# Two decoder layers on one core: more buffers for the split probabilities, and another order of the second phase

## The reference

```
x += tanh(g0) * fp8_product(ln(x), ctx)                      # 128-blocks, quantised and back
x += tanh(f0) * ternary_linear(rms(ln(x)) in 8 bits, W)      # one scale over all rows
x += tanh(g1) * attention(q=ln(x), k=ctx, v=ctx, 8 heads)    # softmax(q^T k / sqrt(d)) over 1024
x += tanh(f1) * sum_e combine[:, e] * (ln(x) @ Wa[e] @ Wb[e])  # top 2 of 8 experts, rank 128
```

## Time and profile before

| | us |
|---|---|
| median of 3 runs | 2032.5 (2029.92 to 2034.0) |
| the profiled execution | 2032.83 |
| its span, first to last instruction | 2031.0 |
| PE busy | 1856.8 |
| DVE busy | 1542.6 |
| ACT busy | 1265.5 |
| POOL busy | 773.8 |

### The profile page before, as it was taken

The page is one execution under the profiler, slowest core; times in us unless marked ns, Lnnn a source line. Parts: engine busy times, 40 slices in busy tenths (PEclk is TensorE's granted clock), DMA queues, the critical chain, the costliest instruction groups (busy, mean ns, idle before and its releaser), DMA issues.

```text
span 2031.0 us, 26460 instructions
## 1 busy us (share of the span) xinstructions
PE 1856.8 (91%) x8968; PEld 838.4 (41%) x8968; DVE 1542.6 (76%) x2386; ACT 1265.5 (62%) x2045; POOL 773.8 (38%) x1100
## 2 busy tenths in 40 slices
PE   1699999894799999999999999999999999999997
PEld 0244444341344444444444444444444444444443
DVE  8899999888777777777777777777777777777662
ACT  4698898666556566656555565656565665555650
POOL 3555565333333333333333333333333333333320
PEclk9999999997999999999999999999999999999999
DMA  9687876796878888887788787888878878888772
GB/s 213 160 208 205 220 204 182 193 228 186 159 150 166 167 164 158 164 168 161 157 165 168 161 159 151 166 167 162 160 156 168 167 152 165 163 171 160 126 145 63
DMA packets 923975, 340.50 MB, mean 168 GB/s; under 512 B 849728, under 2 KB 898880, under 8 KB 923840
## 3 DMA queue, kind: packets, MB, share of 16 engines
q1 hardware_dynamic: 923840, 338.81, 79.6%
HBM read 93.36 MB, written 33.55 MB: 62 GB/s over the span
## 4 chain that ended last, share of the span: by engine, by line
DVE 21%; ACT 20%; issue 20%; POOL 10%; PE 7%; DMA 5%; SPq 0%; ACTq 0%; DVEq 0%; POOLq 0%
ACT slot L885 9%; DVE tiny L1586 7%; ACT arena L872 6%; POOL tiny L710 5%; DVE tiny L1220 4%; POOL tiny L708 4%; DVE slot L1591 3%; DMA probs<-slot 3%; ACT tiny L864 3%; DVE arena L1601 2%; ACT slot L909 2%; DVE slot L1559 2%; DMA slot<-slot 2%; DVE slot L1648 1%; DVE slot L1553 1%
## 5 line engine op out<-in xcount | busy, mean ns | idle before, releaser
L1591 DVE SCALAR_TENSOR_TENSOR slot<-arena,tiny,slot 128x1024 f16<-128x1024 f32 x256 | 328.2, 1282 | 306.0 <-ACT slot L885 305.9
L885 ACT ACTIVATE slot<-arena,tiny 128x1024 f16<-128x1024 f32 x256 | 293.6, 1147 | 174.1 <-POOL tiny L710 155.0
L1083 PE MATMUL sc<-arena,slot 128*128 128x512 f16 x1536 | 371.2, 382 | 19.2 <-ACT arena L872 17.0
L708 POOL TENSOR_SCALAR tiny<-tiny 128x1 f32<-128x1 f32 x256 | 100.1, 391 | 689.8 <-ACT arena L872 689.8
L1586 DVE TENSOR_REDUCE tiny<-sc 128x1 f32<-128x1024 f32 x256 | 306.5, 1207 | 16.5 <-PE sc L1083 15.1
L872 ACT ACTIVATE arena<-sc,tiny,head_tab 128x1024 f32<-128x1024 f32 x256 | 308.1, 1204 | 8.6
L864 ACT ACTIVATE tiny<-tiny,head_tab 128x1 f32<-128x1 f32 x256 | 73.9, 289 | 338.1 <-DVE tiny L1586 338.0
L1083 PEld LDWEIGHTS sc<-arena,slot 128*128 128x128 f16 x1536 | 150.1, 98 | 204.8 <-ACT arena L872 19.5
L1104 PE MATMUL accs<-probs,arena 128*128 128x512 f16 x512 | 196.9, 385 | 23.3 <-issue 21.1
L1106 PE MATMUL accs<-probs,arena 128*128 128x512 f16 x512 | 196.8, 384 | 0.0
L1105 PE MATMUL accs<-probs,arena 128*128 128x512 f16 x512 | 196.6, 384 | 0.0
(11 more groups left out here) (214 smaller groups left out, 2900.9 us busy)
## 6 DMA issues: line engine op xcount, KB each, us to landing
arena<-in_x SPq DMA_DIRECT2D x32, 512.0 KB, 4.2
x_scratch<-arena SPq DMA_DIRECT2D x32, 512.0 KB, 3.7
slot<-x_scratch SPq DMA_DIRECT2D x32, 512.0 KB, 4.1
slot<-in_ctx SPq DMA_DIRECT2D x32, 512.0 KB, 4.5
out<-arena SPq DMA_DIRECT2D x31, 512.0 KB, 3.4
slot<-in_L_ffn_Wa SPq DMA_DIRECT2D x12, 512.0 KB, 5.0
slot<-in_L_ffn_Wb SPq DMA_DIRECT2D x9, 512.0 KB, 4.9
wb_hi<-in_ctx SPq DMA_DIRECT2D x64, 64.0 KB, 2.5
```

What stands on the lines that cost most here:

```text
L885: act.activation(high, full, ACT.Identity, scale=rinv[c % 4][:]).then_inc(s_ph.sem, 1)
L1083: mm = pe.matmul(sc[:, c % 2, h * HALF:(h + 1) * HALF], q[i][:, c * P:(c + 1) * P], k[j][:, h * HALF:(h + 1) * HALF], start=start, stop=stop)
L1591: dve.scalar_tensor_tensor(out=low, in0=full, scalar=rinv[c % 4][:], in1=high, op0=ALU.mult, op1=ALU.subtract).then_inc(s_pl.sem, 1)
```

## The change

Three SBUF tensors of 128 x 1024 f32 are added (`late0` to `late2`). Room for them comes from the argument `dynamic_dma_scratch_size=4096` of the program, which makes the reserved descriptor scratch smaller. `P2` then has four buffers for all tiles and `PF` three; the semaphores of the probability transposes become four, and the waits of `exp` and `prob_high` follow: `exp(n, c)` waits for `prob_low` of the chunk three before, `prob_high(n, c)` for the transpose of the chunk four before. A wait of `finish_x3` in tile 0 goes, since tile 0 no longer borrows x3's buffer for it. The order of all five lists in the loop changes. In the steady rounds the new lists are (the tile is n where none is given):

The diff, with unchanged lines left out and indents shortened:

```diff
...
+late = [sb(f"late{i}", [P, D]) for i in range(3)]
...
-P2, T42 = [slot[i][:].bitcast(F16) for i in (12, 13)], slot[10][:].bitcast(F16)
+P2 = [t[:].bitcast(F16) for t in (slot[12], slot[13], late[0], late[1])]
+T42 = slot[10][:].bitcast(F16)
...
-P2_FIRST = P2 + [slot[i][:].bitcast(F16) for i in (10, 11)]
...
-PF, X3 = (pf[:, 0], pf[:, 1]), (pf[:, 2], pf[:, 3])
-PF_FIRST = PF + X3
+PF, X3 = (pf[:, 0], pf[:, 1], late[2][:]), (pf[:, 2], pf[:, 3])
+PF_FIRST = PF + X3[1:]
...
-        full, both = PF_FIRST[c % 4], P2_FIRST[c % 4]
+        full = PF_FIRST[c % 4]
...
-        full, both = PF[c % 2], P2[c % 2]
+        full = PF[(KB * n + c) % 3]
+    both = P2[c % 4]
...
-s_pt = signal("s_pt0", 16 * KB // 2), signal("s_pt1", 16 * KB // 2)
-s_pt_first = signals("s_pt_first", 4, 32)
+s_pt = signals("s_pt", 4, 32)
...
-        turned = s_pt_first[c % 4] if n == 0 else s_pt[c % 2]
...
-          .then_inc(turned.sem, 16)
+          .then_inc(s_pt[c % 4].sem, 16)
...
+        if quant:
+            load_x1(n + 2)
...
-        if is_x(n + 2) and n >= -1:
-            load_k(n + 2)
-        if cur:
-            turn_probs(n, 1)
-        if is_x(n + 2) and n >= 1:
-            load_x1(n + 2)
...
+            turn_probs(n, 1)
+        if quant:
+            load_k(n + 2)
+        if cur:
...
-            turn_probs(n, 3)
...
+        if cur:
+            turn_probs(n, 3)
...
+            turn_probs(n, 6)
...
-        if cur:
-            turn_probs(n, 6)
...
+        if prev:
+            ln_factors(n - 1, l4_st, l4_p, mv4, a4, rs4, nb4)
+        if cur:
+            row_factor(n, 2)
...
-        if prev:
-            ln_factors(n - 1, l4_st, l4_p, mv4, a4, rs4, nb4)
-        if cur:
-            row_factor(n, 2)
+        if cur:
+            row_factor(n, 3)
+            row_factor(n, 4)
...
-        if cur:
-            row_factor(n, 3)
-            row_factor(n, 4)
-        if prev and cur:
-            hidden_low(n - 1, 0)
...
+            hidden_low(n - 1, 0)
+        if cur:
+            row_factor(n, 7)
+        if prev and cur:
...
-        if cur:
-            row_factor(n, 7)
...
-        elif c >= 2:
-            act.wait_ge(s_pl.sem, s_pl.at(n, c - 1))
+        elif n == 1 and c == 0:
+            act.wait_ge(s_pl.sem, s_pl.at(0, KB - 1))
...
-            act.wait_ge(s_pl.sem, s_pl.at(n - 1, KB - 1 + c))
+            act.wait_ge(s_pl.sem, s_pl.at(n, c - 2))
...
-        chunks = s_pt[c % 2]
-        if n == 0 and c >= 4:
-            act.wait_ge(s_pt_first[c % 4].sem, 16)
-        if n == 1 and c < 2:
-            act.wait_ge(s_pt_first[c].sem, 32)
-        if n > 1 or n == 1 and c >= 2:
-            act.wait_ge(chunks.sem, chunks.at(n - 1, 16 * (c // 2)))
+        if n > 0 or c >= 4:
+            act.wait_ge(s_pt[c % 4].sem, s_pt[c % 4].at(n, 16 * (c // 4)))
...
+            exp(n, 1)
...
-            exp(n, 1)
...
+            query_high(n + 1)
...
-        if nxt:
-            query_high(n + 1)
-        if cur:
-            exp(n, 2)
...
+            exp(n, 2)
+            exp(n, 3)
...
-            exp(n, 3)
+            exp(n, 4)
...
-            exp(n, 4)
+            prob_high(n, 4)
+            exp(n, 5)
+            exp(n, 6)
...
-            prob_high(n, 4)
+            prob_high(n, 5)
+            exp(n, 7)
+            prob_high(n, 6)
...
-        if cur:
-            exp(n, 5)
-            prob_high(n, 5)
-            exp(n, 6)
-        if prev:
...
-            prob_high(n, 6)
-            exp(n, 7)
...
+            for chunks in s_pt:
+                pe.wait_ge(chunks.sem, chunks.at(n, 16 * (h + 1)))
...
-                for chunks in s_pt_first:
-                    pe.wait_ge(chunks.sem, 16 * (h + 1))
...
-            else:
-                for chunks in s_pt:
-                    pe.wait_ge(chunks.sem, chunks.at(n - 1, 32 * (h + 1)))
...
+            scores(n, 3)
...
-        if cur:
-            scores(n, 3)
-        if before:
-            output(n - 2, 1, every)
+            output(n - 2, 1, early)
...
+        if before:
+            output(n - 2, 1, late)
+        if cur:
+            scores(n, 6)
...
-            hidden(n - 1, 0, every)
-            hidden(n - 1, 1, early)
-        if cur:
-            scores(n, 6)
+            hidden(n - 1, 0, early)
+        if cur:
+            scores(n, 7)
...
-            hidden(n - 1, 1, late)
-        if cur:
-            scores(n, 7)
+            hidden(n - 1, 0, late)
+            hidden(n - 1, 1, every)
+        if cur:
...
-        if n == 0:
-            dve.wait_ge(s_pl.sem, s_pl.at(0))
...
+            stats_x3(n - 1, 0)
...
-        if prev:
-            stats_x3(n - 1, 0)
...
-            prob_low(n, 0)
-        if nxt:
-            key_low(n + 1)
-        if cur:
-            prob_low(n, 1)
...
+            prob_low(n, 0)
...
+            row_maxima(n, 3)
...
-        if cur:
-            row_maxima(n, 3)
...
+            prob_low(n, 1)
+        if nxt:
+            key_low(n + 1)
+        if cur:
+            row_maxima(n, 4)
+            row_maxima(n, 5)
...
-        if cur:
-            prob_low(n, 3)
-        if quant:
-            quantise_round(n + 2)
-        if cur:
-            row_maxima(n, 4)
...
+        if cur:
+            row_maxima(n, 6)
+            prob_low(n, 3)
+        if quant:
+            quantise_round(n + 2)
...
+            row_maxima(n, 7)
...
+            prob_low(n, 5)
...
-            row_maxima(n, 5)
-            row_maxima(n, 6)
-            prob_low(n, 5)
+            prob_low(n, 6)
...
-        if cur:
-            row_maxima(n, 7)
-            prob_low(n, 6)
...
-    nc = _bacc.Bacc("TRN2", target_bir_lowering=False, num_devices=1)
+    nc = _bacc.Bacc("TRN2", target_bir_lowering=False, num_devices=1, dynamic_dma_scratch_size=4096)
...
```

More of the change, by code:

```diff
@@ L728, in _ @@
                     row_factor(n, 1)
-                if nxt:
-                    query_low(n + 1)
                 if prev:
@@ L734, in _ @@
                     row_factor(n, 2)
-                if prev:
-                    row_norm(n - 1)
+                if nxt:
+                    query_low(n + 1)
                 if cur:
@@ L739, in _ @@
                     row_factor(n, 4)
-                if prev and cur:
-                    hidden_low(n - 1, 0)
+                if prev:
+                    row_norm(n - 1)
                 if cur:
@@ L745, in _ @@
                 if prev and cur:
-                    hidden_low(n - 1, 1)
+                    hidden_low(n - 1, 0)
                 if cur:
                     row_factor(n, 7)
+                if prev and cur:
+                    hidden_low(n - 1, 1)
         @block.scalar
@@ L1194, in _ @@
                     scores(n, 5)
-                if prev:
-                    router(n - 1)
-                    hidden(n - 1, 0, every)
-                    hidden(n - 1, 1, early)
+                if before:
+                    output(n - 2, 1, late)
                 if cur:
@@ L1201, in _ @@
                 if prev:
-                    hidden(n - 1, 1, late)
+                    router(n - 1)
+                    hidden(n - 1, 0, early)
                 if cur:
                     scores(n, 7)
+                if prev:
+                    hidden(n - 1, 0, late)
+                    hidden(n - 1, 1, every)
+                if cur:
                     values(n, 0, every)
```

## The result

The changed kernel takes 2043.4 us in the median of four runs (2039.35 to 2044.93), the kernel before 2031.2: 1.0057 times as long, 95% interval 1.0038 to 1.0076. It was forecast at 1991 us, and is slower instead. Its profiled execution, 2039.35 us with a span of 2037.6, is the fastest of the four.

What follows compares the result with a forecast made beforehand. PE was taken as the bound: 29 rounds x (47.14 - 45.3 - 0.5) = 38.9 us, plus 2.7 at the ends, 41.6 off 2032.5, gives 1991 us (1984 to 2000, chance 0.52; wider range 1974 to 2016).

Steps and rivals of the forecast that it cites:

- The bound and the floor: Steady rounds 2 to 30: PE bounds the kernel; without its two waits a round takes 45.3 us instead of 47.14.
- The router's wait goes: PE before the router: turn_rows lands at 26.1 us into the round, slot 28.15, so covered by 2 us.
- The values' wait goes: PE before the values' second half: probability chunk 7 lands 6 to 7.5 us into the next round, slot 8.65.
- The new waits before scores 4 and 5: PE waits for exponentials 2 and 3, exponential 2 being behind rows_high: 0.25 us late, then 0.15 more.
- Scores 6: PE waits for exponential 4, which ends at 26.8 us into the round; the shifted slot is 27.25.
- the values behind the weighing: First half of the values needs weigh_hidden 0, done at 40.1 to 40.4 us; slot 40.2, or 40.6 shifted.
- The step that failed: Scores 7 on PE wait for exponential 5, behind prob_high 3 and 4 and POOL's factor 4: 31.5 for slot 31.55.
- A: Slower rival: exponentials starve PE, from exponential 2 behind rows_full; decides at 1.84 us, 3 us a round gives 2063; chance 0.08.
- The lock: POOL's factor steps beside two-tensor DVE work: rows_full 1.0 us later, giving nearly all of the 0.5 us a round.
- The buffers: More probability buffers take away 16 us of ACT transpose waits over 29 rounds, all beside PE; priced at nothing by itself.
- The scratch: Smaller descriptor scratch: POOL issues no DMA, so nothing taken; if SP's queue narrowed, nothing to 0.4 us a round.
- The ends: Outside the steady rounds: round 1 saves about 0.5 us, round 31 2.5, round 32 costs 0.3; together -2.7.

Runs made afterwards that it cites:

- the best version: Changed kernel with prob_low 0 ahead of x3's second half and exponential 5 ahead of prob_high 3 and 4; 1973.2 us, 0.9706 of the kernel before.

## Why the prediction was wrong

- **The bound and the floor** were right: 45.3 us was worked out, 45.30 is reached, with PE busy for 1310.73 of 1311 us.
- **The router's wait goes**: right. rows_full starts 4.0 us behind the values' end (1055.99 to 1059.98), as said. **The values' wait goes**: right. Chunk 7 lands 6.7 us into the round (6 to 7.5 forecast), ahead of its slot at 8.6.
- **The new waits before scores 4 and 5**: 0.25 and 0.15 forecast, 0.29 and 0.21 measured. **Scores 6** and **the values behind the weighing**: no wait forecast beyond those, none measured.
- **The step that failed** is the one that reads "S7 waits for exponential 5, behind prob_high 3 and 4, two bias steps and POOL's factor of chunk 4 ...: 31.5 for 31.55". The slot was right (1073.58 is 31.57 into the round). Exponential 5 ended 33.2 into it. I followed ACT's list and asked of POOL only for factor 4; I did not carry POOL's own list forward, with query_low moved from in front of ln_factors to in front of factor 3. Factor 3 so had its own chain: exponential 2, stretched factor 2 (2.5 to the next start), query_low (2.1), stretched factor 3 (3.1). The row of the stretch was in hand, and I applied it to one step and not to these. The step was sized at 0 and measured 1.76 us, 51 us over 29 rounds. Its own term, factor 4 under quantise_full, was too small as well: with factor 3 out of the way, it alone holds scores 7 for 0.59 to 0.63 us. Without it, as the kernel with exponential 5 early shows, the time is 1990.2, beside the 1991 that was forecast.
- **The rivals.** A had the right kind and point of decision (exponentials starve PE, above 1.84 us a round; 2.25 came), the chance of 0.08 was far too low, and its place, exponential 2 behind rows_full, was wrong: it carries only 0.5 us. I had listed four places with under 0.5 us of room and still held the waits to 0.5 in sum.
- **The lock.** The Trainium skill, SBUF — State Buffer, "SBUF: two separate sides", has the rule of an exclusive lock between GpSimd and a DVE operation with two SBUF inputs. The trace agrees, 1.11 us with prob_low 0 beside the step and 0.19 without. I used it where it changed 1 us and should have asked it of every POOL step in the path.
- **The buffers** were put at nothing and give 6 us by themselves: the prediction took all of ACT's transpose waits to lie beside PE, but the rounds with them were the long ones. **The scratch** at nothing is confirmed.
- **The ends** were put at -2.7 us, and the two profiled executions differ by -5.9 there. This tests little. The kernel with the scratch alone has the lists of before, and its round 2 starts 1.6 us later and the stretch from the start of round 31 on is 3.2 us shorter. In it round 31 idles about as long in front of the values (2.35 us), and the clock stays up in the 7 us behind, where the earlier trace rows had 0.76:

```profile
1944.00:1951.00 7.00, 6.95 (x33) 3.20 (x34) 4.07 (x5) 2.94 (x5) 0.79 (x2) 1.00 0.69 133
```

So the clock's part of the 2.5 us taken for round 31 does not come in every execution.

## What to carry to other kernels

When an order is made denser, carry the list of every in-order engine forward, the least busy one too: POOL was busy for 41% of the changed kernel's span and set the round. A tiny instruction in the path is read at its longest row, not its mean, once a neighbour may lie beside it. And where one late step stands in front of another engine's critical one, changing their order on the engine between them (exponential 5 ahead of prob_high 3) can be worth as much as making the late step early: it took all of the 1.76 us, query_low early took 1.17.

## What the runs showed of the hardware

One-column POOL instructions of 0.22 and 0.57 us took 1.11 and 1.46 us where they started beside a DVE operation on two 128x1024 SBUF tensors (1057.84, 1064.93). Where a second DVE operation in SBUF stood right behind it, they took up to 1.72 (in the best version, at 640.46) and 1.86 (1055.18). Beside a single-tensor scaling in SBUF alone, DVE's L1444 from 637.70 to 638.45 in the kernel before, the 0.57 became 1.05:

```profile
637.83 1.05 POOL L710 TENSOR_TENSOR tiny<-tiny,neg_one 128x1 f32<-128x1 f32 x1
```

Beside maxima read from PSUM they kept their length (1056.73, 0.22).

PE's idle time of 1.64 us in every steady round left the granted clock at 1.00, while one of 2.97 us was followed by 7.1 us at a mean of 0.58. A stall of 1.76 us from start to start cost no more than itself; one of 3.13 cost most of 5.75. The length of one idle time does not decide alone: the first of these stalls (PE starts again at 598.4) and the 2.35 us in round 31 of the scratch-only kernel left the clock at 1.00, and 2.39 us in the kernel before were followed by 0.76.
